# Reordering TensorE's work inside a pipelined local attention: value projection, output product and query turns

## The chip, the core and the metric

The kernel runs on one core of one Trainium2 chip. The metric is the device time of a whole execution in microseconds (us). Inside the core, TensorE (PE, with its weight loads shown apart as PEld), VectorE (DVE), ScalarE (ACT) and GpSimd (POOL) each run their own instruction stream in order and wait for one another only through counting semaphores. SyncE (SP) issues the transfers.

## The reference

An array x of 16 sequences of 256 tokens with 128 channels passes through four residual blocks: a linear attention, a block "ffn", a column attention, and the "ffn" block again with the same weights. Each is applied to a layer norm of x. The changed code is in the "ffn" block, which is two layers deep (so four such layers run, n = 0 to 3):

```
for l in range(DEPTH):                       # DEPTH = 2
    h = shift_token(x)
    q, k, v = split(h @ wqkv)                # 8 heads of 64
    q, k = l2norm(q) * qs, l2norm(k) * ksc
    q, k = rotary_xpos(q, k)
    o = local_attention(q, k, v)             # windows of 64 tokens, each sees itself and the one before
    x = x + o @ wo
    h = layernorm(shift_token(x)) * lg + lb
    a, g = split(h @ w1 + b1)
    x = x + (a * gelu(g)) @ w2 + b2
```

## The kernel before

Each of the four layers first runs its token attention (`attention_programs`) and then its gated part (`gated_programs`). The attention works through 32 tiles. For projection, a tile is 128 tokens with all 8 heads; for attention itself, tile i is a pair of heads (c = i % 4) of a pair of sequences (p = i // 4). Each engine has a hand-written loop over i in which tile i is in one phase and later tiles are in earlier phases (LEAD = 5, LATE = 27). In one pass of TensorE's loop:

- `query_key(i + 5)`: queries and keys of a later tile projected into the two banks `proj`, three products each.
- `scores(i)`: masks, then 32 small products (64 x 64 tiles of the array) into the two banks `sc`.
- `values(i + 3)`: the value projection, three products into the bank `ob`. This bank is also where `attend` writes, so `values(i + 3, i)` first waits on `f_ot` until the attention output of tile i - 2 has been copied out of it.
- `turn_probabilities(i - 1)`: eight transposes of the normalised probabilities, four for each half e of the tile (e is one of the two heads), half 0 into `pt[0]` and half 1 into `pt[1]`.
- `project(i - 2)`: the output product with Wo, into the bank `ss`. It needs the same copied output.
- `turn_tile(.., 1)`: keys transposed into `pt[1]`, once ScalarE has copied half 1 of the probabilities from there (`f_p1`).
- `attend(i - 1)`: 24 products of values by probabilities into `ob`, once both halves have been copied (`f_p0` by VectorE, `f_p1` by ScalarE).
- `turn_tile(.., 0)`: queries transposed into `pt[0]`.

In passes with i % 4 == 0, scores come behind values already. In the passes after LATE there is no later tile to project, scores run one tile ahead, and the first steps of the next part (`gate_centre`, `gate_variance`) are woven in.

ScalarE's pass i up to i = 26 is, in program order: squares of the projection (L506), copy of the values (L516), copy of half 1 of the probabilities of tile i - 1 (L916), the eight exponentials of tile i with their sums (L908), copy of the output of tile i - 1 out of `ob` (L922, `f_ot`), copy of the queries (L526), and two short operations for the inverse norms (L926, L930). At i = 27 the copy of the queries comes ahead of that of the output. From i = 29 on the exponentials of tile i and the copy of the output of tile i - 2 come ahead of the copy of the probabilities of tile i - 1.

VectorE's pass holds rotary products (L452, L462), score maxima (L824), the copy of half 0 of the probabilities (L830), sums of squares (L473, L477), the inverse of the softmax sums (L839) and the copy of the keys (L487). GpSimd's pass holds the normalisation of the probabilities (L993), the scaling of queries and keys (L545) and the rotary sums (L536). ScalarE, VectorE and SyncE programs are not part of the diff; GpSimd's `scale` is.

In the layers n = 0 and n = 2 the loop starts at i = -6 with a ramp of projections and turned tiles; in n = 1 and n = 3 this ramp lies in the gated part of the layer before (`early`).

Of the kernel before, what the change touches and what calls it, by code (L numbers as in the profile page):

```python
# [326 lines left out]
TILES = 4 * PAIRS  # L327
LEAD = 5
FIRST, LAST = -LEAD - 1, TILES + 2
LATE = TILES - LEAD  # L330

tokens = lambda t: slice(t * P, (t + 1) * P)
# [101 lines left out]
        split_product(pe, K, banks[w][:], q, t, w).then_inc(S.f_q, 1)  # L434


def transposes(pe, K, n, j, w, bank):

    S = K.s
    pe.wait_ge(S.f_scl, 2 * TILES * n + 2 * j + (2, 1)[w])  # L440
    for c in range(CHUNKS):
        mm = pe.transpose(bank[:, tokens(c)], K.sm[:, j % 2, w, tokens(c)], K.ident[:])  # L442
    mm.then_inc((S.f_ttq, S.f_ttk)[w], 1)
# [92 lines left out]
        pool.tensor_tensor(K.sm[:, r, w], K.m1[:, r, w], K.m2[:, r, w], ALU.add).then_inc(S.f_sum, 1)  # L536


def scale(pool, K, n, j):

    S, r = K.s, j % 2
    for w in (1, 0):
        pool.wait_ge(S.f_sum, 2 * TILES * n + 2 * j + w + 1)
        pool.wait_ge(S.f_rn, TILES * n + j + 1)
        pool.tensor_tensor(heads(K.sm[:, r, w]), heads(K.sm[:, r, w]),  # L545
                           K.rnt[:, r, w * HEADS:(w + 1) * HEADS].unsqueeze(2).broadcast_to([P, HEADS, DH]),
                           ALU.mult).then_inc(S.f_scl, 1)
# [92 lines left out]
def attention_programs(K, n):  # L640

    S = K.s
    pt = K.pt
# [33 lines left out]
    def tensor(pe):  # L677
# [9 lines left out]
        def values(m, i):  # L687
            if m == 0 and begin < 0:
                pe.wait_ge(S.wa_lo, 3 * (n + 1))
                pe.wait_ge(S.ln_nrm, entry + 6)  # L690
            if i >= 2:
                pe.wait_ge(S.f_ot, TILES * n + i - 1)
            elif m >= 1:
                pe.wait_ge(S.f_ve, TILES * n + m)
            split_product(pe, K, K.ob[:], m // 4, m % 4, 2).then_inc(S.f_v, 1)
# [29 lines left out]
                        if s == 1 and w == 2:  # L725
                            mm.then_inc(S.f_sc, 1)

        def turn_probabilities(i):
            for e in range(2):
                pe.wait_ge(S.f_pn, 2 * TILES * n + 2 * i + e + 1)  # L730
                pe.wait_ge((S.f_tq, S.f_tk)[e], TILES * n + min(i + LEAD, TILES))
                for k in range(4):
                    mm = pe.transpose(pt[e][:, tokens(k)], K.prob[:, i % 2, e, k], K.ident[:])  # L733
                mm.then_inc(S.f_pt, 1)

        def attend(i):
            p, c = divmod(i, 4)
# [18 lines left out]
        def turn_tile(i, j, w):  # L756
            if j == 0:
                pe.wait_ge(S.ln_nrm, entry + 5)
            if i >= 1:
                pe.wait_ge((S.f_p0, S.f_p1)[w], TILES * n + i)  # L760
            elif j >= 1:
                pe.wait_ge((S.f_tq, S.f_tk)[w], TILES * n + j)
            transposes(pe, K, n, j, w, pt[w])

        def project(i):
            p, c = divmod(i, 4)
            pe.wait_ge(S.f_ot, TILES * n + i + 1)
            if i == 0:
                pe.wait_ge(S.wa_wo, 16 * (n + 1))
            if c == 0 and p >= 1:  # L770
                pe.wait_ge(S.f_y, PAIRS * n + p)
            pe.matmul(K.ss[:], K.wo[:, c], K.ot[:, c], start=(c == 0), stop=(c == CHUNKS - 1)).then_inc(S.f_wo, 1)  # L772
# [6 lines left out]
        for i in range(begin, LAST):  # L779
            if (1 if begin < 0 else 0) <= i + LEAD < TILES:  # L780
                query_key(pe, K, n, i + LEAD, K.proj)
            if due(i) is not None:
                if due(i) + 2 < PAIRS:
                    centre(due(i) + 2)
                variance(due(i))
            if 0 <= i <= LATE and i % 4:
                scores(i)
            if LATE < i < TILES - 1:
                scores(i + 1)
            if 0 <= i + 3 < TILES:  # L790
                values(i + 3, i)
            if 0 <= i <= LATE and i % 4 == 0:
                scores(i)
            if 1 <= i <= TILES:
                turn_probabilities(i - 1)
            if 2 <= i:
                project(i - 2)
            if 0 <= i + LEAD - 1 < TILES:
                turn_tile(i, i + LEAD - 1, 1)
            if 1 <= i <= TILES:  # L800
                attend(i - 1)
            if 0 <= i + LEAD - 1 < TILES:
                turn_tile(i, i + LEAD - 1, 0)
            if i == LATE:
                scores(i + 1)
            if i == TILES - 2:
                gate_centre(pe, K, n, 0)
            if i == TILES - 1:
                gate_variance(pe, K, n, 0)
                gate_centre(pe, K, n, 1)  # L810
            if i == TILES:
                gate_variance(pe, K, n, 1)
                gate_centre(pe, K, n, 2)
# [174 lines left out]
    def gpsimd(pool):  # L988
        def normalise(i):
            r = i % 2  # L990
            for e in range(2):
                pool.wait_ge(S.f_rd, TILES * n + i + 1)
                pool.tensor_tensor(K.prob[:, r, e], K.prob[:, r, e], K.rden[:, r, e].unsqueeze(2).broadcast_to([P, 4, P]),  # L993
                                   ALU.mult).then_inc(S.f_pn, 1)

        if begin < 0:
            pool.memset(K.ss16[:], NORM_MIN).then_inc(S.f_floor, 1)
            split_value_weights(pool, K, n)
            low_parts(pool, K, n, 1)
        for i in range(begin, LAST):  # L1000
            j = i + LEAD
            if 1 <= i <= TILES:
                normalise(i - 1)
            if 0 <= j - 1 < TILES:
                scale(pool, K, n, j - 1)
            if i % 4 == 1 and 1 <= i and i // 4 + 2 < PAIRS:
                low_parts(pool, K, n, i // 4 + 2)
            if 0 <= j < TILES:
                sums(pool, K, n, j)
            if i == TILES - LEAD:  # L1010
                split_mlp_weights(pool, K, n)
            if i == TILES - 4:
                pool.wait_ge(S.f_sc, 2 * TILES * n + 2 * (TILES - 4))
                pool.wait_ge(S.f_pn, 2 * TILES * n + 2 * i)
                pool.memset(first_rows[:, 0:PAIRS], 0.0).then_inc(S.g_z, 1)
                pool.wait_ge(S.g_z, 2 * n + 1)
            if i == TILES - 1:
                pool.wait_ge(S.f_sc, 2 * TILES * (n + 1))
                pool.wait_ge(S.f_pn, 2 * TILES * n + 2 * i)
                pool.memset(first_rows[:, PAIRS:2 * PAIRS], 0.0).then_inc(S.g_z, 1)  # L1020
                pool.wait_ge(S.g_z, 2 * n + 2)
# [4 lines left out]
def gated_programs(K, n):  # L1026

    S = K.s
# [25 lines left out]
    def gpsimd(pool):  # L1054
        if last:
            for p in range(PAIRS):
                pool.wait_ge(S.f_y, PAIRS * n + p + 1)
                pool.tensor_tensor(K.X[:, pair(p)], K.X[:, pair(p)], K.Y[:, pair(p)], ALU.add).then_inc(S.f_xy, 1)
        if (n + 1) % DEPTH:
            split_query_key_weights(pool, K, n + 1)  # L1060
            low_parts(pool, K, n + 1, 0)
            scale_tables(pool, K, n + 1)
            split_value_weights(pool, K, n + 1)
            for j in range(LEAD):
                if j == 2:
                    low_parts(pool, K, n + 1, 1)
                sums(pool, K, n + 1, j)
                pool.wait_ge(S.f_cl, TILES * (n + 1) + j + 1)
                pool.tensor_tensor(K.rnt[:, j % 2], K.ssc[:], K.mhalf[:].broadcast_to([P, 2 * HEADS]), ALU.pow).then_inc(S.f_rn, 1)
                if j < LEAD - 1:  # L1070
                    scale(pool, K, n + 1, j)

    def tensor(pe):
        def up(x):
# [31 lines left out]
        def early(x):  # L1106
            s, r = divmod(x - 7, 3)
            if r == 0 and 0 <= s < LEAD:
                if s == 0:
                    pe.wait_ge(S.wa_lo, 3 * (n + 1) + 2)  # L1110
                query_key(pe, K, n + 1, s, K.pt)
            if x in (11, 12, 13):
                if x == 11:
                    pe.wait_ge(S.wa_lo, 3 * (n + 2))
                else:
                    pe.wait_ge(S.f_ve, TILES * (n + 1) + x - 11)
                split_product(pe, K, K.ss[:], 0, x - 11, 2).then_inc(S.f_v, 1)
            if 2 <= s < LEAD + 1 and r == 1:
                if s == 2:
                    pe.wait_ge(S.f_ve, TILES * (n + 1) + 3)  # L1120
                else:
                    pe.wait_ge(S.f_tq, TILES * (n + 1) + s - 2)
                transposes(pe, K, n + 1, s - 2, 1, K.ss)
            if 2 <= s < LEAD + 1 and r == 2:
                pe.wait_ge(S.f_tk, TILES * (n + 1) + s - 1)
                transposes(pe, K, n + 1, s - 2, 0, K.ss)

        def turn_output(p):
            pe.wait_ge(S.ff_y, PAIRS * n + p + 1)
# [1268 lines left out]
```

## Time and profile before

| | |
|---|---|
| median of 3 runs | 1757.11 us (1752.05 to 1757.42) |
| the profiled execution | 1754.2 us, span 1752.4 us, mean granted TensorE clock 0.993 |
| busy, share of the span | PE 96%, PEld 62%, DVE 77%, ACT 75%, POOL 64% |
| core of each token attention | tiles 4 to 24, 147.8 to 147.9 us for 20 passes, in each of the four layers |

The span is the time from the first to the last instruction; some 2 us of the execution's time lie around it. The timeline view lists instructions with their start, their duration, the engine, the line, output<-input, and in brackets how long the engine stood idle before and what released it. PE and PEld are two rows of one engine; matmul ends are modelled, so starts are the safer reading.

### The profile page before, as it was taken

How to read it: one execution, taken by the hardware profiler on the slowest of the kernel's cores; microseconds unless marked ns; L12 is line 12 of the kernel's file. 1: busy time of each engine (PE TensorE's matmuls, PEld its weight loads, DVE VectorE, ACT ScalarE, POOL GpSimd, SP SyncE). 2: the span in 40 equal slices, each digit the busy share in tenths (PEclk: the TensorE clock that was granted, in tenths of full speed). 3: DMA queues.
4: the chain of work that ended last, by engine and by line, in shares of the span. 5: the costliest groups of instructions: out<-in, count | busy, mean ns of one | idle time of the engine just before them, and what ended most of it. 6: DMA issues, size and time to landing. Idle time of an engine off the chain costs nothing. (4 is left out here: it accounts for less than half of the span.)

```text
span 1752.4 us, 43496 instructions
## 1 busy us (share of the span) xinstructions
PE 1676.7 (96%) x15560; PEld 1090.1 (62%) x15560; DVE 1342.6 (77%) x2369; ACT 1305.6 (75%) x4472; POOL 1121.3 (64%) x1012
## 2 busy tenths in 40 slices
PE   8998899999989999999899999899999989999999
PEld 5664677775657777554444444577776557777655
DVE  5556898984778988456789887889885678898654
ACT  5445788887358888745799998788887538888863
POOL 5556999992579999703322221899995378999730
PEclk9999999999999999999899999999999999999999
DMA  3001111103011110201665553111102102110111
GB/s 91 2 2 43 27 31 26 26 20 88 13 37 26 32 26 20 56 15 35 124 102 100 104 94 59 48 26 32 26 20 56 52 12 44 26 32 20 44 31 42
DMA packets 67309, 74.90 MB, mean 43 GB/s; under 512 B 13380, under 2 KB 50968, under 8 KB 65048
## 3 DMA queue, kind: packets, MB, share of 16 engines
q1 hardware_dynamic: 67096, 72.13, 19.3%
q8 instruction: 125, 2.05, 0.5%
q14 instruction: 88, 0.72, 0.1%
HBM read 28.08 MB, written 10.49 MB: 22 GB/s over the span
## 5 line engine op out<-in xcount | busy, mean ns | idle before, releaser
L536 POOL TENSOR_TENSOR rsum<-pa,pb 128x512 f32<-128x512 f32 x256 | 325.6, 1292 | 63.8 <-DVE pa L452 42.3
L908 ACT ACTIVATE ffn_prob<-sc,ffn_nmax 128x128 f32<-128x128 f32 x928 | 326.7, 387 | 4.1 <-DVE ffn_nmax L824 4.1
L993 POOL TENSOR_TENSOR ffn_prob<-ffn_prob,ffn_rden 128x512 f32<-128x512 f32 x256 | 265.2, 1057 | 52.0 <-DVE ffn_rden L839 44.5
L545 POOL TENSOR_TENSOR rsum<-rsum,ffn_rnt 128x512 f32<-128x512 f32 x256 | 261.4, 1042 | 8.0 <-ACT ffn_rnt L930 5.7
L462 DVE TENSOR_TENSOR pb<-proj,tab 128x512 f32<-128x512 f32 x236 | 161.9, 686 | 85.8 <-ACT rn L506 85.4
L908 ACT ACTIVATION_READ_ACCUMULATOR ffn_prob<-sc,ffn_nmax 128x1 f32 x928 | 210.3, 227 | 0.0
L442 PE MATMUL pt<-ident,rsum 128*128 128x128 f32 x960 | 154.2, 284 | 10.4 <-POOL rsum L545 7.7
L442 PEld LDWEIGHTS pt<-ident,rsum 128*128 128x128 f32 x960 | 100.7, 141 | 91.8 <-ACT ffn_ptb L916 70.5
L824 DVE TENSOR_REDUCE ffn_nmax<-sc 128x4 f32<-128x512 f32 x232 | 148.6, 682 | 11.8 <-PE sc L723 8.5
L473 DVE TENSOR_REDUCE ffn_ss<-rn 128x16 f32<-128x1024 f32 x128 | 154.7, 1209 | 0.0
L452 DVE TENSOR_TENSOR pa<-proj,tab 128x512 f32<-128x512 f32 x236 | 150.9, 681 | 0.0
L733 PE MATMUL pt<-ident,ffn_prob 128*128 128x128 f32 x1024 | 143.2, 277 | 6.3 <-POOL ffn_prob L993 5.7
L752 PEld LDWEIGHTS ob<-ffn_ptb,ffn_v 128*64 128x64 f32 x3072 | 126.0, 137 | 33.2 <-issue 20.9
L752 PE MATMUL ob<-ffn_ptb,ffn_v 128*64 128x64 f32 (+1 forms) x3072 | 143.6, 243 | 0.0
L733 PEld LDWEIGHTS pt<-ident,ffn_prob 128*128 128x128 f32 x1024 | 115.7, 140 | 39.7 <-POOL ffn_prob L993 24.7
L2072 ACT ACTIVATE column_E<-proj,column_nm 128x256 f32<-128x256 f32 x256 | 122.3, 500 | 16.9 <-DVE column_nm L1966 16.3
L1168 ACT ACTIVATE ffn_prob<-proj,ffn_colb 128x512 f32<-128x512 f32 (+1 forms) x92 | 62.5, 687 | 96.6 <-PE proj L1093 95.4
L772 PE MATMUL ss<-ffn_ot,ffn_wo 128*128 128x512 f32 x256 | 131.9, 597 | 0.8 <-ACT ffn_ot L922 0.8
L1814 POOL CAST column_kh<-column_ks 128x2048 fp32r<-128x2048 f32 x16 | 30.6, 1910 | 150.9 <-DMA column_ks<-qk_parts 141.2
L506 ACT ACTIVATE rn<-proj 128x512 f32<-128x512 f32 x236 | 125.8, 582 | 0.4
L1205 DVE SCALAR_TENSOR_TENSOR ffn_ptb<-sc,ffn_colb,ffn_prob 128x512 f32<-128x512 f32 (+1 forms) x92 | 68.4, 747 | 73.6 <-ACT ffn_prob L1168 66.9
L2072 ACT ACTIVATE column_E<-sc,column_nm 128x256 f32<-128x256 f32 x256 | 123.2, 511 | 0.0
(322 smaller groups left out, 4348.7 us busy)
## 6 DMA issues: line engine op xcount, KB each, us to landing
ffn_v<-ffn_v SPq DMA_DIRECT2D x128, 128.0 KB, 2.3
column_ks<-qk_parts SPq DMA_DIRECT2D x64, 128.0 KB, 4.0
rn<-Y SPq DMA_DIRECT2D x32, 128.0 KB, 2.3
qk_parts<-column_hi SPq DMA_DIRECT2D x64, 64.0 KB, 1.6
qk_parts<-column_lo SPq DMA_DIRECT2D x64, 64.0 KB, 1.6
column_qs<-qk_parts SPq DMA_DIRECT2D x32, 128.0 KB
column_qs<-qk_parts SPq DMA_DIRECT2D x64, 64.0 KB
rn<-Y SPq DMA_DIRECT2D x32, 127.5 KB, 2.4
```

The costliest lines, as they stand in the source:

```text
L442: mm = pe.transpose(bank[:, tokens(c)], K.sm[:, j % 2, w, tokens(c)], K.ident[:])
L452: return dve.tensor_tensor(heads(K.m1[:, r, w]), heads(banks[w][:]), K.tab[:, t % 2, 2 * w].unsqueeze(1).broadcast_to([P, HEADS, DH]), ALU ...
L462: return dve.tensor_tensor(halves(K.m2[:, r, w]), halves(banks[w][:])[:, :, ::-1], K.tab[:, t % 2, 2 * w + 1].rearrange("p (a d) -> p a d" ...
L473: dve.tensor_reduce(K.ss16[:, :, 0], K.sq.rearrange("p w (h d) -> p (w h) d", d=DH), AX.X, ALU.add).then_inc(S.f_ss, 1)
L536: pool.tensor_tensor(K.sm[:, r, w], K.m1[:, r, w], K.m2[:, r, w], ALU.add).then_inc(S.f_sum, 1)
L545: pool.tensor_tensor(heads(K.sm[:, r, w]), heads(K.sm[:, r, w]), K.rnt[:, r, w * HEADS:(w + 1) * HEADS].unsqueeze(2).broadcast_to([P, HEAD ...
L733: mm = pe.transpose(pt[e][:, tokens(k)], K.prob[:, i % 2, e, k], K.ident[:])
L752: mm = pe.matmul(K.ob[e * DH:(e + 1) * DH, s * SEQ + q0:s * SEQ + q1], K.v[:, b, 3 * s + k, hc], K.ptb[:, r, e, blk, q], start=True, stop= ...
L824: dve.tensor_reduce(K.nmax[:, i % 2, e], blocks(score_banks(i)[e][:]), AX.X, ALU.max, negate=True).then_inc(S.f_mx, 1)
L908: ins = act.activation(K.prob[:, r, e, k], score_banks(i)[e][:, tokens(k)], ACT.Exp, bias=K.nmax[:, r, e, k:k + 1], accum_out=K.den[:, r, ...
L993: pool.tensor_tensor(K.prob[:, r, e], K.prob[:, r, e], K.rden[:, r, e].unsqueeze(2).broadcast_to([P, 4, P]), ALU.mult).then_inc(S.f_pn, 1)
L2072: act.activation(B.E[:, slot, bt], score_banks[c][:, bt * SEQ:(bt + 1) * SEQ], ACT.Exp, bias=B.nm[:, slot, bt:bt + 1], accum_out=B.dn[:, s ...
```

## The change

Four orders change, and no operation is added, removed or resized:

- in TensorE's pass, `values` comes ahead of `scores` in every pass, not only when i % 4 == 0 (also ahead of the scores that run one tile ahead behind LATE)
- `turn_probabilities` is cut in two, with `project` between half 0 and half 1
- the queries are turned ahead of `attend`, and the keys behind it (they were the other way round)
- `scale` on GpSimd scales queries before keys in the attention loop, to match; the tiles prepared in the gated part keep keys first, through the new argument `first`

```diff
-def transposes(pe, K, n, j, w, bank):
+def transposes(pe, K, n, j, w, bank, first):
...
-    pe.wait_ge(S.f_scl, 2 * TILES * n + 2 * j + (2, 1)[w])
+    pe.wait_ge(S.f_scl, 2 * TILES * n + 2 * j + (1 if w == first else 2))
...
-def scale(pool, K, n, j):
+def scale(pool, K, n, j, first):
...
-    for w in (1, 0):
+    for w in (first, 1 - first):
...
-        def turn_probabilities(i):
-            for e in range(2):
-                pe.wait_ge(S.f_pn, 2 * TILES * n + 2 * i + e + 1)
-                pe.wait_ge((S.f_tq, S.f_tk)[e], TILES * n + min(i + LEAD, TILES))
-                for k in range(4):
-                    mm = pe.transpose(pt[e][:, tokens(k)], K.prob[:, i % 2, e, k], K.ident[:])
-                mm.then_inc(S.f_pt, 1)
+        def turn_probabilities(i, e):
+            pe.wait_ge(S.f_pn, 2 * TILES * n + 2 * i + e + 1)
+            pe.wait_ge((S.f_tq, S.f_tk)[e], TILES * n + min(i + LEAD, TILES))
+            for k in range(4):
+                mm = pe.transpose(pt[e][:, tokens(k)], K.prob[:, i % 2, e, k], K.ident[:])
+            mm.then_inc(S.f_pt, 1)
...
-            transposes(pe, K, n, j, w, pt[w])
+            transposes(pe, K, n, j, w, pt[w], 0)
...
-            if 0 <= i <= LATE and i % 4:
+            if 0 <= i + 3 < TILES:
+                values(i + 3, i)
+            if 0 <= i <= LATE:
                 scores(i)
             if LATE < i < TILES - 1:
                 scores(i + 1)
-            if 0 <= i + 3 < TILES:
-                values(i + 3, i)
-            if 0 <= i <= LATE and i % 4 == 0:
-                scores(i)
             if 1 <= i <= TILES:
-                turn_probabilities(i - 1)
+                turn_probabilities(i - 1, 0)
             if 2 <= i:
                 project(i - 2)
+            if 1 <= i <= TILES:
+                turn_probabilities(i - 1, 1)
             if 0 <= i + LEAD - 1 < TILES:
-                turn_tile(i, i + LEAD - 1, 1)
+                turn_tile(i, i + LEAD - 1, 0)
             if 1 <= i <= TILES:
                 attend(i - 1)
             if 0 <= i + LEAD - 1 < TILES:
-                turn_tile(i, i + LEAD - 1, 0)
+                turn_tile(i, i + LEAD - 1, 1)
...
-                scale(pool, K, n, j - 1)
+                scale(pool, K, n, j - 1, 0)
...
-                    scale(pool, K, n + 1, j)
+                    scale(pool, K, n + 1, j, 1)
...
-                transposes(pe, K, n + 1, s - 2, 1, K.ss)
+                transposes(pe, K, n + 1, s - 2, 1, K.ss, 1)
...
-                transposes(pe, K, n + 1, s - 2, 0, K.ss)
+                transposes(pe, K, n + 1, s - 2, 0, K.ss, 1)
```

## Rows read from the trace of the kernel before

**Rows 1.** Windows, passes 4 to 24: length, busy PE PEld DVE ACT POOL, PEclk

```profile
215.22:363.06 147.84, 147.84 (x1741) 110.04 (x1740) 132.50 (x231) 127.83 (x481) 137.89 (x125) 1.00 0.12 27
```

**Rows 2.** Waits in the second layer's attention: who for whom, total, times, longest

```profile
PEld pt L442 <- ACT ffn_ptb L916: 12.2, 19, 0.6
ACT ffn_ptb L916 <- PE pt L733: 9.6, 19, 1.0
ACT ffn_v L516 <- PE ob L422: 8.7, 14, 0.6
```

**Rows 3.** Timeline of pass 13 of the second layer, scores ahead of values

```profile
602.48 0.64 ACT L922 COPY ffn_ot<-ob 128x512 f32<-128x512 f32 x1
...
604.72 0.19 PEld L420 LDWEIGHTS ob<-ffn_wv_hi,ffn_hhi 128*128 128x128 f32 x1 [0.17 <-issue]
...
605.06 0.40 PE L421 MATMUL ob<-ffn_wv_lo,ffn_hhi 128*128 128x512 f32 x1
...
605.54 1.04 PE L733 MATMUL pt<-ident,ffn_prob 128*128 128x128 f32 x8
...
606.41 1.02 PE L772 MATMUL ss<-ffn_ot,ffn_wo 128*128 128x512 f32 x2
...
607.25 0.42 PEld L442 LDWEIGHTS pt<-ident,rsum 128*128 128x128 f32 x4 [0.64 <-ACT ffn_ptb L916]
```

**Rows 4.** Timeline of pass 16 of the second layer, values ahead of scores

```profile
624.20 0.19 PEld L420 LDWEIGHTS proj<-wqk_hi,ffn_hhi 128*128 128x128 f32 x1
...
624.77 0.64 ACT L922 COPY ffn_ot<-ob 128x512 f32<-128x512 f32 x1
...
625.47 0.19 PEld L420 LDWEIGHTS ob<-ffn_wv_hi,ffn_hhi 128*128 128x128 f32 x1
...
625.94 0.40 PE L421 MATMUL ob<-ffn_wv_lo,ffn_hhi 128*128 128x512 f32 x1
...
627.71 0.85 PEld L733 LDWEIGHTS pt<-ident,ffn_prob 128*128 128x128 f32 x8 [0.17 <-POOL ffn_prob L993]
...
628.64 1.02 PE L772 MATMUL ss<-ffn_ot,ffn_wo 128*128 128x512 f32 x2
628.84 0.58 ACT L916 COPY ffn_ptb<-pt 128x512 f32<-128x512 f32 x1 [0.96 <-PE pt L733]
629.05 0.68 DVE L830 COPY ffn_ptb<-pt 128x512 f32<-128x512 f32 x1
...
629.48 0.42 PEld L442 LDWEIGHTS pt<-ident,rsum 128*128 128x128 f32 x4 [0.64 <-ACT ffn_ptb L916]
629.50 0.63 PE L442 MATMUL pt<-ident,rsum 128*128 128x128 f32 x4
...
630.06 0.98 PEld L752 LDWEIGHTS ob<-ffn_ptb,ffn_v 128*64 128x64 f32 x24 [0.17 <-issue]
...
631.50 0.19 PEld L420 LDWEIGHTS proj<-wqk_hi,ffn_hhi 128*128 128x128 f32 x1
...
632.07 0.64 ACT L922 COPY ffn_ot<-ob 128x512 f32<-128x512 f32 x1
```

**Rows 5.** Timeline of ScalarE in pass 1 of the second layer

```profile
520.96 0.63 ACT L922 COPY ffn_ot<-ob 128x512 f32<-128x512 f32 x1
```

**Rows 6.** Timeline of the second layer's last passes, 27 to 32

```profile
713.35 0.11 PEld L713 LDWEIGHTS sc<-mask,identb 64*64 64x64 bf16 x4 [1.22 <-ACT ffn_qT L526]
...
717.53 0.58 ACT L916 COPY ffn_ptb<-pt 128x512 f32<-128x512 f32 x1 [0.29 <-PE pt L733]
...
723.50 0.69 ACT L922 COPY ffn_ot<-ob 128x512 f32<-128x512 f32 x1
...
733.11 0.59 ACT L916 COPY ffn_ptb<-pt 128x512 f32<-128x512 f32 x1 [0.15 <-PE pt L733]
...
738.77 0.98 PEld L752 LDWEIGHTS ob<-ffn_ptb,ffn_v 128*64 128x64 f32 x24 [0.76 <-DVE ffn_ptb L830]
```

**Rows 7.** Windows, a stretch of the column attention, same columns

```profile
800.00:900.00 100.00, 90.46 (x484) 42.21 (x484) 73.75 (x148) 77.70 (x278) 35.05 (x28) 0.90 0.49 90
```

## The prediction

> **What bounds the kernel now.** I read the windows over the steady passes first. Twenty passes take 147.84 us in the first layer (147.84 to 147.89 in the others), 7.39 us each, and TensorE's matmul row is busy all of it at full granted clock, while GpSimd is at 93%, VectorE at 90% and ScalarE at 86% [rows 1]. No engine has a tenth to spare, so the kernel is a ring of engines that hand tiles on, and the question is which ring of waits is the longest.
>
> The waits view comes second. The reader sees that TensorE's weight loads wait most for ScalarE's copy of probability half 1 before the keys are turned, and that ScalarE waits for TensorE in two places, 9.6 us before that copy and 8.7 us before the copy of the values [rows 2]. These look like gaps to close. The timeline tells what they are worth. In pass 13 the eight turns start at 605.54, the output product at 606.41 and the keys' load at 607.25 [rows 3]: 0.87 and then 0.84. Pass 16 shows the product followed by the keys' turn after 0.84 as well, with the same 0.64 of load wait [rows 4]. The product itself has two parts whose row of pass 13 is 1.02 long, so the 0.64 lies beside a running product: the weight loader is idle, the array is not. ScalarE's two gaps are off the ring too. TensorE is bound by its own order, and ScalarE's copy lands just in time.
>
> **The slack between the rings.** `values` may start only when the output of the tile before has left `ob`. In pass 13, where scores come first, the output copy ends at 602.48 + 0.64 = 603.12 and the values start at 604.72: 1.6 us of slack [rows 3]. In pass 16, where values already come first, the copy ends at 625.41 and the values start at 625.47 [rows 4]. That is 0.06 us. So the new order of values and scores uses up all the slack that there is, in every pass, though by itself it costs nothing: pass 16 is of that kind now and is not slower.
>
> **The edits one by one.** (Times relative to the load of the first value product, V.)
>
> *Values ahead of scores.* Work on the array is the same. Pass 16 has V at 625.47, the turns of half 0 at 627.71 and all eight turns done when the output product starts at 628.64, so at V + 3.17 [rows 4]. ScalarE gets its values sooner, but it had been waiting there (8.7 us over 14 waits [rows 2]), and behind it waits again for the probabilities. Gain: none.
>
> *Output product between the halves.* Half 0 is unaffected. Half 1 is finished one output product later. Its length is the step from its start to that of the keys' turn, 629.50 - 628.64 = 0.86 [rows 4]. Nothing on TensorE gets longer, but what waits for half 1 is late by 0.86: ScalarE's copy L916 starts 0.20 after the last turn (628.64 to 628.84) [rows 4], so now at V + 3.17 + 0.86 + 0.20 = V + 4.23. Queued behind that copy on ScalarE are the eight exponentials of the next tile and then the copy of the output out of `ob`, and for that one the next `values` waits. The possible gain, that half 1 no longer waits for GpSimd's second normalisation, is small: that wait is 0.17 in its row of pass 16 [rows 4], and the array was draining anyway.
>
> *Queries before, keys behind `attend`.* The queries' turn has to wait for VectorE's copy of half 0, which in pass 16 starts at 629.05, V + 3.58 [rows 4]. `attend` needs ScalarE's copy, done at V + 4.23 + 0.58 = V + 4.81. Before, the whole output product lay in the time between the last turn and this copy; now only the queries' turn (about 0.4) does, and TensorE stands for some 0.3 us. Keys arrive 1.5 us later at VectorE, whose copy of them stands late in its pass behind other work, so that costs nothing; if that cover were gone it would cost up to that 1.5 only in the pass that begins a new group of four heads. `scale` in the other order costs GpSimd the same work; the first half it gives out is the one now wanted first. No transfer is moved past another: SyncE's stores of values follow the values' copy and come a little sooner.
>
> **The ring that closes.** V, then scores, half 0, product, half 1 up to ScalarE's copy: 4.23. Copy and exponentials until the output copy starts: 632.07 - 628.84 = 3.23; the output copy 0.64; its release to TensorE 0.06 (copy of half 1 ends 629.42, the load that it releases is at 629.48) [rows 4]. Together 8.16. When values wait, the array is empty and no load is hidden under another product, yet the second product follows sooner: V to the second value product is 0.34 in pass 13 and 0.47 in pass 16 [rows 3, 4]. That takes 0.13 off: **8.03 us per pass**, against 7.39 now. Before, the way from V to the end of the turns was 1.69 (604.72 to 606.41 [rows 3]) in place of 4.03, so the same ring was 5.8 and never closed. The other engines have room: their work per pass is 6.9 (GpSimd), 6.6 (VectorE) and 6.4 us (ScalarE) [rows 1].
>
> By how many passes: the output copy of pass 1 starts at 520.96 in the second layer [rows 5] and should not move, since half 1 of the first tile waits for GpSimd there. It releases values of pass 2 at about 521.65. Twenty-five turns of 8.03 later, at 722.4, come the values of pass 27. In that pass scores of the next tile wait for the queries' copy, behind the exponentials: 4.10 + 3.23 + 0.63 + 0.05 = 8.01, so at 730.4. They stand at 713.35 [rows 6]. **Loss up to there 17.1 us per layer.**
>
> *The last passes.* From that point on, ScalarE copied half 1 of tile 27 4.18 later; now it is 0.86 (product) and about 0.2 (two more changes between the full array and its 64 x 64 tiles, at 0.17 of idle loads each [rows 3], partly hidden) later. Then 5.97 to the output copy (717.53 to 723.50) [rows 6]. In the old order half 1 was turned by then. Now the output product waits for the output copy and half 1 for the product: 0.69 + 0.05 + 0.86 + 0.44 (four turns) + 0.20 = 2.24 before the next copy of half 1. Two more passes of 2.24 + 3.23 put the copy of half 1 of tile 30 at 24.4 behind the scores, where it is 19.8 now (733.11) [rows 6]: 4.6 later. The last `attend` (738.77) adds 0.4. **Loss 5.0 per layer**; bounds 1.0 (only the product is felt once) to 7.
>
> Sum: (17.1 + 5.0) x 4 = 88. The profiled execution took 1754.2, its span 1752.4; that makes 1842.6. The median of runs is 2.9 above the profiled one, so 1845.
>
> **A rule weighed.** The turns, the copies and the product use three banks. The Trainium skill, Perfetto Trace Analysis, section Optimizing Tensor Performance (Matmuls), says that independent groups should rotate through banks so that the copying of one overlaps the products of the next. The new order does just that between `pt[0]`, `ss` and `pt[1]`, and by the rule alone the 0.64 of load wait would be the gain. The rows say that the array was covered there.
>
> **Rivals.**
> 1. *The order relieves TensorE* (the other side; the rule above speaks for it). ScalarE would not hold the ring, because something in its 3.87 shrinks. Then every pass is like pass 16, 7.30 between its loads of the query projection (624.20 to 631.50 [rows 4]) against 7.39, and GpSimd's late half 1 no longer counts: 0.09 x 25 x 4 = 9 us less, 1748. It decides if the output copy ends less than 1.27 us into the pass (624.20 to 625.47), as now. Against: the copy of half 1 cannot start before half 1 is turned. Chance 0.05.
> 2. *Only `attend` waits, the `ob` ring does not close.* TensorE's order with the wait for half 1: 4.87 to `attend`, 1.44 for it and the turn behind it (630.06 to 631.50), 1.27 for the query projection [rows 4]: 7.58 per pass. 0.19 x 25 x 4 = 19, with the last passes 39: 1796. It decides if exponentials and copies after half 1 take under 3.3 us instead of 3.87. Chance 0.08.
> 3. *Nothing measurable*: the delays fall into ScalarE's two gaps, 1757. They did amount to 18.3 us in 140 us [rows 2], about 1 us per pass, but they stand before the copy that is late, not behind it. Chance 0.03.
> 4. *TensorE's clock drops* in the new gaps. It is granted in full in the steady windows [rows 1], and was granted at 0.90 over 100 us of the column attention [rows 7]. At 0.90 the array's 7.39 becomes 8.2, 0.2 above the ring: 20 more, 1865; at 1.2 GHz throughout it would be far over. Chance 0.04.
>
> **How the numbers follow.** The forecast has 0.80. A measurement of this kernel can tell about 0.3%, 5 us. The ring's own uncertainty is 0.15 us per pass (15 us in all), the last passes' -4 to +2 per layer (-16 to +8): the forecast's range is 1820 to 1868. For 8 in 10 with the rivals I take 1812 to 1868. Faster 0.05, same 0.03, slower 0.92.
>
> **What the profile would show.** The output copy L922 released straight before the first value product, with "ACT ffn_ot" as the releaser of PE's L420, 0.4 to 0.7 us each pass; `attend` (L752's place) waiting some 0.3 for ScalarE's L916; twenty passes in about 160.6 us; TensorE's load share down from 74% to 68%; the gap of ScalarE before its values' copy gone and the one before its copy of half 1 larger. The forecast is wrong if the passes stay under 7.6 us or if TensorE shows no wait on L922.

## The result: 1845.89 us, 5.25% slower

| | median us | range | runs |
|---|---|---|---|
| before | 1754.58 | 1751.97 to 1757.42 | 4 |
| changed | 1845.89 | 1843.94 to 1851.46 | 4 |

The ratio is 1.0525, 95% interval 1.051 to 1.054. The profiled execution of the changed kernel took 1851.46 us (span 1849.7), 5.6 above the median; the section on the hardware tells where that comes from. The kernel before, measured again beside it, has a median of 1754.58, against 1757.11 when the prediction was made.

Lines of the page of the changed kernel (engine totals, then groups of instructions: busy us, mean ns | idle before). From `turn_probabilities` on (L733 in the kernel before) line numbers are one lower in the changed kernel; in the kernels of the experiments they can differ by one or two more.

```profile
PE 1724.2 (93%) x15560; PEld 1100.1 (59%) x15560; DVE 1358.3 (73%) x2369; ACT 1296.6 (70%) x4472; POOL 1123.0 (61%) x1012
...
L915 ACT COPY ffn_ptb<-pt 128x512 f32<-128x512 f32 x128 | 75.0, 586 | 221.9 <-PE pt L732 221.9
...
L771 PE MATMUL ss<-ffn_ot,ffn_wo 128*128 128x512 f32 x256 | 133.5, 603 | 6.2 <-ACT ffn_ot L921 6.2
```

ScalarE stands idle for 221.9 us before its copies of the probabilities, waiting for TensorE's turns, and TensorE's busy share has gone from 96% to 93%.

The window over passes 4 to 24 of the second layer (length, then busy PE, PEld, DVE, ACT, POOL, and PEclk):

```profile
567.23:727.49 160.26, 155.30 (x1740) 110.12 (x1740) 135.71 (x231) 126.24 (x481) 138.32 (x126) 1.00 0.11 25
```

It is 160.26 us against the 147.84 of [rows 1] (first layer; the second layer's passes have the same length): 8.01 us per pass, with the same count of matmuls and weight loads and the clock granted in full. Nothing was added; every engine became idler.

The waits view of the second layer's attention (600 to 740 us: who for whom, total, times, longest):

```profile
ACT ffn_ptb L915 <- PE pt L732: 30.0, 18, 1.7
...
PEld ob L420 <- ACT ffn_ot L921: 8.9, 17, 0.6
...
PEld pt L442 <- DVE ffn_ptb L829: 6.5, 18, 0.4
```

Beside [rows 2], the wait of the values' load (L420) for ScalarE's output copy (L921) is new, 17 times, and the load of the turn behind the halves now waits for VectorE's copy of half 0. ScalarE's wait for the turns has trebled (9.6 to 30.0). The loads' share of the window of twenty passes is 69% where it was 74%.

One sign that the prediction named is missing: `attend` is not listed as waiting for ScalarE. In the timeline below its load (652.11) starts 0.17 behind the queries' loads and 0.08 behind the end of ScalarE's copy (652.03). The wait stands one step earlier, before the queries' turn, and it is for VectorE.

The timeline of one pass of the changed kernel, against [rows 4]:

```profile
647.35 0.19 PEld L420 LDWEIGHTS ob<-ffn_wv_hi,ffn_hhi 128*128 128x128 f32 x1 [0.41 <-ACT ffn_ot L921]
...
647.69 0.40 PE L421 MATMUL ob<-ffn_wv_lo,ffn_hhi 128*128 128x512 f32 x1
...
649.45 0.42 PEld L732 LDWEIGHTS pt<-ident,ffn_prob 128*128 128x128 f32 x4 [0.17 <-issue]
...
649.95 1.02 PE L771 MATMUL ss<-ffn_ot,ffn_wo 128*128 128x512 f32 x2
...
650.79 0.68 DVE L829 COPY ffn_ptb<-pt 128x512 f32<-128x512 f32 x1
650.81 0.60 PE L732 MATMUL pt<-ident,ffn_prob 128*128 128x128 f32 x4
...
651.44 0.59 ACT L915 COPY ffn_ptb<-pt 128x512 f32<-128x512 f32 x1 [1.67 <-PE pt L732]
651.53 0.42 PEld L442 LDWEIGHTS pt<-ident,rsum 128*128 128x128 f32 x4 [0.36 <-DVE ffn_ptb L829]
...
652.11 1.00 PEld L751 LDWEIGHTS ob<-ffn_ptb,ffn_v 128*64 128x64 f32 x24 [0.17 <-issue]
...
653.57 0.19 PEld L420 LDWEIGHTS proj<-wqk_hi,ffn_hhi 128*128 128x128 f32 x1
...
654.67 0.63 ACT L921 COPY ffn_ot<-ob 128x512 f32<-128x512 f32 x1
...
655.36 0.19 PEld L420 LDWEIGHTS ob<-ffn_wv_hi,ffn_hhi 128*128 128x128 f32 x1 [0.56 <-ACT ffn_ot L921]
```

The reader can walk the ring in it. Values start at 647.35. Half 0 is turned from 649.45, the product runs from 649.95, half 1 comes 0.86 behind it (650.81), and ScalarE gets it at 651.44: 4.09 after the values. 3.23 later, at 654.67, the exponentials are through and the output copy starts; it ends at 655.30 and the next values start at 655.36. 4.09 + 3.23 + 0.63 + 0.06 = 8.01.

The last passes of the same layer on ScalarE, against [rows 6]:

```profile
764.86 0.58 ACT L915 COPY ffn_ptb<-pt 128x512 f32<-128x512 f32 x1 [2.51 <-PE pt L732]
...
770.82 0.69 ACT L921 COPY ffn_ot<-ob 128x512 f32<-128x512 f32 x1
773.16 0.58 ACT L915 COPY ffn_ptb<-pt 128x512 f32<-128x512 f32 x1 [1.65 <-PE pt L732]
...
776.39 0.63 ACT L921 COPY ffn_ot<-ob 128x512 f32<-128x512 f32 x1
778.68 0.59 ACT L915 COPY ffn_ptb<-pt 128x512 f32<-128x512 f32 x1 [1.65 <-PE pt L732]
...
784.20 0.58 ACT L915 COPY ffn_ptb<-pt 128x512 f32<-128x512 f32 x1 [1.65 <-PE pt L732]
```

From the copy of half 1 of tile 27 (764.86) to that of tile 30 (784.20) are 19.3 us; before, 717.53 to 733.11 were 15.6 [rows 6].

### The profile page after: what moved, and what is told of

It reads as the page before. It is cut to its first block and busy times, and to the rows that moved or that the text cites. A ratio compares the mean times of both kernels' runs of the same rounds, so it can differ in the third digit from the quotient of the medians.

```text
span 1849.7 us, 43496 instructions
## 1 busy us (share of the span) xinstructions
PE 1724.2 (93%) x15560; PEld 1100.1 (59%) x15560; DVE 1358.3 (73%) x2369; ACT 1296.6 (70%) x4472; POOL 1123.0 (61%) x1012
## 5 line engine op out<-in xcount | busy, mean ns | idle before, releaser
L915 ACT COPY ffn_ptb<-pt 128x512 f32<-128x512 f32 x128 | 75.0, 586 | 221.9 <-PE pt L732 221.9
L732 PEld LDWEIGHTS pt<-ident,ffn_prob 128*128 128x128 f32 x1024 | 119.4, 142 | 94.2 <-issue 86.5
L732 PE MATMUL pt<-ident,ffn_prob 128*128 128x128 f32 x1024 | 162.5, 282 | 1.6 <-POOL ffn_prob L992 1.2
L723 PE MATMUL sc<-ffn_kT,ffn_qT 64*64 64x128 f32 (+1 forms) x3712 | 123.0, 261 | 0.0
```

## The experiments

The three edits on TensorE make eight combinations. All are in the table; six more kernels, told below it, move something else. "Pass" is the mean of 20 passes of the second layer, read from the starts of ScalarE's probability copies or of the values' loads. Ratios are to the kernel before on the same chip, and each profile is of one execution.

| kernel | pass us | median us | ratio (95%) |
|---|---|---|---|
| before | 7.39 | 1754.6 to 1757.1, by comparison | 1 |
| values first | 7.38 | 1755.28 | 1.0003 (0.9988 to 1.0017) |
| queries first | 7.42 | 1758.36 | 1.0008 (0.9998 to 1.0019) |
| values + queries first | 7.61 | 1775.13 | 1.0113 (1.0093 to 1.0133) |
| product between | 8.20 | 1858.79 | 1.0588 (1.0573 to 1.0603) |
| values first + product between | 8.16 | 1860.76 | 1.0606 (1.0577 to 1.0636) |
| product between + queries first | 7.83 | 1819.67 | 1.0361 (1.0337 to 1.0386) |
| all three (the change) | 8.01 | 1845.89 | 1.0525 (1.051 to 1.054) |

The time grows by a smaller share than the pass, since only some 100 of these passes lie in it and the rest of the kernel did not move.

**Values first.** The order of values and scores of the change, with `turn_probabilities` for both halves together and keys ahead of `attend`. Against the changed kernel:

```diff
-            transposes(pe, K, n, j, w, pt[w], 0)
+            transposes(pe, K, n, j, w, pt[w], 1)
...
             if 1 <= i <= TILES:
                 turn_probabilities(i - 1, 0)
+                turn_probabilities(i - 1, 1)
             if 2 <= i:
                 project(i - 2)
-            if 1 <= i <= TILES:
-                turn_probabilities(i - 1, 1)
...
-                turn_tile(i, i + LEAD - 1, 0)
+                turn_tile(i, i + LEAD - 1, 1)
...
-                turn_tile(i, i + LEAD - 1, 1)
+                turn_tile(i, i + LEAD - 1, 0)
...
-                scale(pool, K, n, j - 1, 0)
+                scale(pool, K, n, j - 1, 1)
```

> Only the values go ahead of the scores; both halves are turned together, keys ahead of attend. Theory of the ring (values wait for the output copy, which waits for the exponentials and for half 1): without the product in front of half 1 the ring is 3.17 + 0.20 + 3.23 + 0.64 + 0.06 = 7.30 us per pass, just what TensorE needs in pass 16, so no loss: 1745 to 1757 us. Rival, that this edit alone brings the waits for the bank: values wait 0.4 us or more in each pass, 1795 us or more.

1755.28 us, no difference. The passes are 7.30, 7.30, 7.62 and 7.30. The ring of 7.30 just fits; the 7.62 stands where GpSimd also splits an input (L554) and the turn of half 1 waits 0.36 for GpSimd's normalisation.

**Product between.** Of the change only the product between the halves stays. Scores come ahead of values as before (i % 4 != 0), and keys ahead of `attend`. Against the changed kernel:

```diff
-            transposes(pe, K, n, j, w, pt[w], 0)
+            transposes(pe, K, n, j, w, pt[w], 1)
...
-            if 0 <= i + 3 < TILES:
-                values(i + 3, i)
-            if 0 <= i <= LATE:
+            if 0 <= i <= LATE and i % 4:
                 scores(i)
             if LATE < i < TILES - 1:
                 scores(i + 1)
+            if 0 <= i + 3 < TILES:
+                values(i + 3, i)
+            if 0 <= i <= LATE and i % 4 == 0:
+                scores(i)
...
-                turn_tile(i, i + LEAD - 1, 0)
+                turn_tile(i, i + LEAD - 1, 1)
...
-                turn_tile(i, i + LEAD - 1, 1)
+                turn_tile(i, i + LEAD - 1, 0)
...
-                scale(pool, K, n, j - 1, 0)
+                scale(pool, K, n, j - 1, 1)
```

> Only the output product goes between the halves; scores ahead of values and keys ahead of attend, as before. Theory of the ring: the ring from values to values is 2.55 + 0.20 + 3.23 + 0.64 + 0.06 = 6.7 us and stays open, so values wait for nothing. But the keys wait for the copy of half 1, and the product no longer lies in that time: half 1 is turned 5.33 us into the pass, copied at 6.17, then keys 0.44 + 0.13, attend 1.05, queries 0.41: 8.2 us per pass, 0.8 x 25 x 4 = 81 and 20 for the last passes, about 1855 us. Rival, that this edit costs only through the ring: 7.39 us per pass, 1757 to 1777 us.

1858.79 us, 8.20 per pass: this edit alone is dearer than all three. The weight loads of this kernel:

```profile
646.63 0.42 PEld L442 LDWEIGHTS pt<-ident,rsum 128*128 128x128 f32 x4 [0.91 <-ACT ffn_ptb L917]
...
648.65 0.19 PEld L420 LDWEIGHTS proj<-wqk_hi,ffn_hhi 128*128 128x128 f32 x1
...
654.85 0.42 PEld L442 LDWEIGHTS pt<-ident,rsum 128*128 128x128 f32 x4 [0.91 <-ACT ffn_ptb L917]
```

The keys' loads wait 0.91 for ScalarE's copy, 17 times, 0.7 of it with the array idle too, and no value load waits for the output copy. 8.22 separate the two loads of the keys.

**Queries first.** Scores ahead of values, both halves together, and the exchange of queries and keys with the order of scaling (the change's own lines for `turn_tile` and `scale`).

> Only the queries go ahead of attend and the keys behind it (with the order of scaling). Theory: the product still covers the copy of half 1, and the queries need VectorE's copy of half 0, which was there in time: no wait, 7.39 us per pass or a little less, 1745 to 1757 us. Rival, that keys are late for VectorE or for the scores of the next group of heads: up to 1 us in each fourth pass, 7 x 4 of them, 1765 to 1785 us.

1758.36 us, no difference. Every fourth step is 7.66: in the pass where values come first as well, the queries' load waits 0.95 for VectorE's copy of half 0. The other three are 7.32, 7.42 and 7.26.

**Output copied midway.** The changed kernel with ScalarE's output copy between the exponentials of half 0 and half 1:

```diff
                 ins.then_inc(S.f_ex, 1)
+                if e == 0 and 1 <= i < LATE:
+                    keep_output(i - 1)
...
-            if 1 <= i < LATE:
-                keep_output(i - 1)
```

> The changed kernel, with one line of ScalarE moved: the output copy stands between the exponentials of half 0 and of half 1 (passes 1 to 26), so it is 1.4 us earlier; nothing on TensorE moves. Theory of the ring: the ring falls to 6.7 us and opens, values wait for nothing, what stays is attend's wait for half 1: 7.58 us per pass, and 20 us of the last passes: about 1796 us. Rival, that the loss lies in TensorE's order (attend, changes of tile size) and the wait of values is only where it shows: 1840 to 1850 us as in the changed kernel.

1837.93 us (ratio 1.0453, 1.0431 to 1.0475). Neither number: 7.92 per pass in the mean, in steps of 7.90, 8.23, 7.62 and 7.93. The timeline of this kernel:

```profile
644.99 0.42 PEld L442 LDWEIGHTS pt<-ident,rsum 128*128 128x128 f32 x4 [0.66 <-DVE ffn_ptb L829]
...
645.58 0.98 PEld L751 LDWEIGHTS ob<-ffn_ptb,ffn_v 128*64 128x64 f32 x24 [0.17 <-issue]
...
646.75 0.59 ACT L923 COPY ffn_ot<-ob 128x512 f32<-128x512 f32 x1
...
648.29 0.19 PEld L420 LDWEIGHTS ob<-ffn_wv_hi,ffn_hhi 128*128 128x128 f32 x1
...
652.89 0.42 PEld L442 LDWEIGHTS pt<-ident,rsum 128*128 128x128 f32 x4 [0.66 <-DVE ffn_ptb L829]
```

The values' load at 648.29 has no wait on ScalarE any more, so the ring did open. But the queries' load now waits 0.66 for VectorE (L829), and the output copy starts only when `attend` has ended. I had built another ring: output copy, exponentials of half 1, queries' copy, inverse norms, squares, VectorE's maxima and its copy of half 0, queries' turn, `attend`, output copy: 646.75 to 654.65 in the trace, 7.90 us. What makes the neighbouring steps longer and shorter was not followed. The run shows that the wait of values goes, but not what the pass would be with nothing in its place.

**Product between and queries first.** The changed kernel with the old condition for scores and values.

> The changed kernel with values behind scores again, as before the change; product between the halves and queries ahead of attend stay. Theory of two waits: without values ahead of scores the ring through the bank is 6.7 us and open; attend still waits for the copy of half 1 at 6.17, so 6.17 + 1.05 + 0.41 = 7.63 us per pass: 1757 + 0.24 x 25 x 4 + 20 = about 1801 us. Rival: values ahead cost nothing, as they cost nothing alone, so 1840 to 1850 us.

1819.67 us. It is some 26 us faster than the full change, so values first, which alone costs nothing, costs 26 us here. It is 18 us above my sum because the steps are 7.68, 8.01, 7.69 and 7.91 in place of 7.63. Every fourth pass has values ahead of scores already, and there the ring closes at its 8.01 (values wait 0.32 for the output copy), which I had not counted. The 7.91 has no such wait. In it, as in every second pass, the queries' loads wait 0.62 for VectorE's copy of half 0, 0.4 of it with the array idle; that was not counted either.

**Values and queries first.** The changed kernel with `turn_probabilities` for both halves together ahead of `project`.

> The changed kernel with the output product behind both halves again; values ahead of scores and queries ahead of attend stay. Theory: half 1 is turned at V + 3.17, the ring is 7.30 us and TensorE needs 7.30 to 7.39: 1745 to 1757 us, no measurable difference from the kernel before or a shade faster. Rival, that the loss needs only values first and the late keys: above 1775 us.

1775.13 us: neither theory, but clear of the kernel before. The loads of this kernel:

```profile
648.04 0.19 PEld L420 LDWEIGHTS ob<-ffn_wv_hi,ffn_hhi 128*128 128x128 f32 x1
...
651.09 0.30 PEld L771 LDWEIGHTS ss<-ffn_ot,ffn_wo 128*128 128x128 f32 x2
652.34 0.42 PEld L442 LDWEIGHTS pt<-ident,rsum 128*128 128x128 f32 x4 [0.95 <-DVE ffn_ptb L828]
...
655.64 0.19 PEld L420 LDWEIGHTS ob<-ffn_wv_hi,ffn_hhi 128*128 128x128 f32 x1
```

The queries' load waits 0.95, against 0.64 that the product covers, and the pass is 7.60 (648.04 to 655.64). VectorE can take the maxima only when the scores are there, 0.7 us later than where scores come first, and copies half 0 behind them; in this kernel its maxima (L822) wait for the scores 16 times in 140 us, 7.9 us in all. In the prediction I had seen that this copy starts at V + 3.58, and priced it at nothing, because the copy of half 1 was later still.

**Old turns at the end.** The changed kernel, but from pass 28 on both halves are turned ahead of the product:

```diff
-            if 2 <= i:
+            if 2 <= i <= LATE:
                 project(i - 2)
             if 1 <= i <= TILES:
                 turn_probabilities(i - 1, 1)
+            if LATE < i:
+                project(i - 2)
```

> The changed kernel, but from pass 28 on the output product stands behind both halves. Theory: the 5 us per layer of the last passes go, 25 passes of 8.0 us stay: 20 us less than the changed kernel, 1826 us. Rival: the last passes are bound by something else (exponentials, gate), 1840 to 1846 us.

1825.32 us (ratio 1.0397, 1.0368 to 1.0427), some 21 below the changed kernel. The time from the probability copy of tile 26 to that of tile 31 falls from 34.06 to 28.85 us; before it was 28.58.

**Queries copied first, on the changed kernel and on the kernel before.** The work stays, and only the order of two ScalarE copies is swapped:

```diff
-            if 1 <= i < LATE:
-                keep_output(i - 1)
             if 0 <= j - 1 < TILES:
                 keep_queries(act, K, n, j - 1, pt[0])
+            if 1 <= i < LATE:
+                keep_output(i - 1)
```

> The changed kernel with two copies of ScalarE swapped in each pass: the queries' copy (0.46 us from start to start) ahead of the output copy. No engine gets more work. Theory: the output copy stands on the ring, so every pass is 0.46 longer, 8.48 us: 46 us more than the changed kernel, about 1892 us. Rival, that TensorE's own order sets the pass and the wait of values is a by-product: within 5 us of the changed kernel.

On the changed kernel 1895.14 us (ratio 1.0792, 1.0759 to 1.0825), 8.50 per pass. Its timeline:

```profile
641.03 0.63 ACT L526 COPY ffn_qT<-pt 128x512 f32<-128x512 f32 x1
...
641.50 0.65 ACT L921 COPY ffn_ot<-ob 128x512 f32<-128x512 f32 x1
...
642.20 0.19 PEld L420 LDWEIGHTS ob<-ffn_wv_hi,ffn_hhi 128*128 128x128 f32 x1 [1.05 <-ACT ffn_ot L921]
...
646.30 0.59 ACT L915 COPY ffn_ptb<-pt 128x512 f32<-128x512 f32 x1 [2.15 <-PE pt L732]
...
650.70 0.19 PEld L420 LDWEIGHTS ob<-ffn_wv_hi,ffn_hhi 128*128 128x128 f32 x1 [1.05 <-ACT ffn_ot L921]
```

The output copy starts 0.47 behind the queries' copy, the values' load waits 1.05 for it, and from values to values it is 642.20 to 650.70 = 8.50, so 0.49 longer than in the changed kernel.

> The kernel before with the same swap of two ScalarE copies as in the run on the changed kernel. Theory of slack: where scores come ahead of values the output copy has 1.6 us to spare, so 0.46 later costs nothing; only in each fourth pass, where values come first, it costs 0.4: 0.4 x 7 x 4 = 11, about 1768 us. Rival, that a later output copy costs 0.46 in every pass whatever the order (ScalarE's order is bound): 1803 us.

On the kernel before 1765.02 us (ratio 1.0058, 1.0045 to 1.0071). Its loads of values:

```profile
626.58 0.19 PEld L420 LDWEIGHTS ob<-ffn_wv_hi,ffn_hhi 128*128 128x128 f32 x1 [0.17 <-issue]
632.88 0.19 PEld L420 LDWEIGHTS ob<-ffn_wv_hi,ffn_hhi 128*128 128x128 f32 x1 [0.52 <-ACT ffn_ot L922]
641.59 0.19 PEld L420 LDWEIGHTS ob<-ffn_wv_hi,ffn_hhi 128*128 128x128 f32 x1 [0.17 <-issue]
```

Only the values of each fourth pass wait for the output copy. The step to them grows from 5.82 to 6.30, and the next one gives 0.13 back. So the same half microsecond costs 47 to 49 us (by ratios, by medians) on one kernel and 10 on the other.

**Values first and product between.** The changed kernel with keys ahead of `attend` and queries behind it.

> The changed kernel with keys ahead of attend and queries behind it again: values first and product between the halves only. Theory: half 1 is turned 1.27 + 4.03 = 5.30 us into the pass, copied at 6.14; only then keys 0.58, attend 1.05, queries 0.38: 8.15 us per pass, above the ring's 8.01, with the last passes about 1855 us. Rival, that the ring through the bank sets the pass whatever is behind the halves: 8.01 us, 1843 to 1847 us.

1860.76 us, 8.16 per pass, equal in every pass. By these sums, of two waits the longer decides: 8.15 for keys and `attend` in a row behind half 1, against the ring's 8.01. So the exchange of queries and keys, alone worth nothing, gives 15 us back in the change.

**Halves swapped.** The changed kernel with TensorE untouched; ScalarE and VectorE exchange the halves that they copy:

```diff
-            dve.wait_ge(S.f_pt, 2 * TILES * n + 2 * i + 1)
+            dve.wait_ge(S.f_pt, 2 * TILES * n + 2 * i + 2)
...
-            dve.tensor_copy(K.ptb[:, i % 2, 0], blocks(pt[0][:])).then_inc(S.f_p0, 1)
+            dve.tensor_copy(K.ptb[:, i % 2, 1], blocks(pt[1][:])).then_inc(S.f_p1, 1)
...
-            act.wait_ge(S.f_pt, 2 * TILES * n + 2 * i + 2)
+            act.wait_ge(S.f_pt, 2 * TILES * n + 2 * i + 1)
...
-            act.copy(K.ptb[:, i % 2, 1], blocks(pt[1][:])).then_inc(S.f_p1, 1)
+            act.copy(K.ptb[:, i % 2, 0], blocks(pt[0][:])).then_inc(S.f_p0, 1)
```

> The changed kernel, TensorE untouched, but ScalarE copies half 0 and VectorE half 1. Work is the same on each engine. Theory of the ring: ScalarE's copy, exponentials and output copy now hang on half 0, turned 1.3 us before half 1, so the ring falls to 6.7 us and opens; attend waits for VectorE's copy of half 1 at V + 4.75: 4.75 + 1.44 + 1.27 = 7.46 us per pass, and most of the last passes' loss goes too: 1765 to 1775 us. Rival, that the product between the halves costs by itself, whoever copies: 1840 us or more.

1814.98 us (ratio 1.0347, 1.0331 to 1.0363), 31 faster than the change and 40 above the upper end of what I expected. Its timeline:

```profile
644.49 0.19 PEld L420 LDWEIGHTS ob<-ffn_wv_hi,ffn_hhi 128*128 128x128 f32 x1
...
647.50 0.59 ACT L915 COPY ffn_ptb<-pt 128x512 f32<-128x512 f32 x1 [0.54 <-PE pt L732]
...
648.16 0.60 PE L732 MATMUL pt<-ident,ffn_prob 128*128 128x128 f32 x4
...
648.79 0.69 DVE L829 COPY ffn_ptb<-pt 128x512 f32<-128x512 f32 x1 [0.57 <-PE pt L732]
...
649.55 1.01 PEld L751 LDWEIGHTS ob<-ffn_ptb,ffn_v 128*64 128x64 f32 x24 [0.60 <-issue]
...
650.74 0.62 ACT L921 COPY ffn_ot<-ob 128x512 f32<-128x512 f32 x1
...
652.29 0.19 PEld L420 LDWEIGHTS ob<-ffn_wv_hi,ffn_hhi 128*128 128x128 f32 x1
```

The ring is open: the output copy ends at 650.74 + 0.62 = 651.36, 0.9 us before the values' load. This pass is 7.80 (644.49 to 652.29), the mean of twenty 7.78, and the rows give my error. Half 1 is turned by V + 4.10, VectorE starts 0.20 later and takes 0.69, so `attend` begins at V + 5.06; I had left out the 0.20 and taken ScalarE's shorter copy. With 1.47 to the next query projection and 1.27 to the values the sum is 7.80. The other part of the miss is the last passes. I had expected most of their loss to go, and none of it did: from the probability copy of tile 26 to that of tile 31 are 33.99 us, against 34.06 in the changed kernel.

**Values and queries first, halves swapped.** The kernel of "values and queries first" with the swap just shown.

> Values first and queries ahead of attend, both halves turned together, and ScalarE copies half 0, VectorE half 1. Theory: the queries' wait for VectorE's copy (7.61 us per pass in the run with both edits) goes, since ScalarE has copied half 0 by V + 3.5; VectorE's copy of half 1 ends at V + 4.25, behind the queries' turn: 7.30 to 7.39 us per pass, 1745 to 1757 us. Rival, that the wait moves on to attend: above 1765 us.

1752.31 us (ratio 0.9984, 0.9975 to 0.9993): passes of 7.27, 7.27, 7.27 and 7.66, mean 7.37. It is the fastest of all and its interval lies just below 1, a gain smaller than the 0.3% that the prediction took as what can be told. The wait for VectorE's copy of half 0 (0.22 us in each pass, 20 us in all) is gone.

## Why the prediction was right

**The ring.** Forecast 8.03 us per pass, measured 8.01. Its terms: 4.10 to ScalarE's copy (4.09), 3.23 (3.23), 0.64 (0.63), 0.06 (0.06). That it is this ring, and not only a wait that shows, rests on the swap of the two copies: 0.47 more on one link made every pass 0.49 longer, at the same work. On the kernel before, whose ring was priced at 5.8 with slack everywhere but in each fourth pass, the same swap costs only there.

The 0.86 for the product, by which half 1 is late, was read from a step whose end was also a wait for ScalarE's copy [rows 4]. That was not safe, but it held: in the changed kernel, where the next turn waits for no other engine, the step is 0.86 as well (649.95 to 650.81).

**Where it starts and ends.** Delay in front of the last passes 17.1 forecast; the probability copy of tile 26 of the second layer moves from 709.43 to 755.63, 46.20, of which 29.25 were there when the layer's values began (507.77 to 537.02): 16.95. The last passes cost 5.2 in the run that undoes them (34.06 against 28.85), forecast 5.0. The whole second layer lost 22.3 (its last `attend` moved 51.57, less 29.25), forecast 22.1. The sum of 1845 stands beside 1845.89, and that it is this near is in part luck. The forecast loss was 88, the measured one 91.3, and the prediction started from a median of 1757.11 where the one measured beside the change is 1754.58.

**The edits one by one.** Values first: nothing gained and nothing lost alone, as said. Product between: the culprit, as said, through half 1 being late by one product. But the prediction tells only one of the two costs of this edit. Without the other edits the ring stays open and the edit costs more (8.20), because the keys and `attend` both stand behind the late copy. The queries' turn, which the prediction priced as leaving TensorE a stall of 0.3, is what shortens this second path to less than the ring.

**What was mis-sized.** VectorE's copy of half 0 was put at nothing. In the change that holds for the time: the queries' turn does wait for it (0.36 of load wait), but ScalarE's copy, on which the ring hangs, does not. The stall of 0.3 that the prediction put before `attend` is not there in the rows. Without the product between it is 0.22 us in each pass (7.61 against 7.39), 20 us: the change would have been slower even without its dear edit. And the price of 7.58 for a pass with the ring opened (second rival) was never met: the two kernels that opened it came to 7.92 and 7.78, each held by a path that the opening itself made or lengthened. What a pass would be with values in a bank of their own no run shows; the banks `proj` (two), `sc` (two), `pt` (two), `ob` and `ss` all have their work.

**The rivals.** Relief of TensorE: ruled out as to the whole change; the 0.64 of load wait before the keys was covered by the product, and where the product was moved away it became 0.91, 0.7 of it with the array idle (product between). The bank-rotation rule of the Trainium skill (Perfetto Trace Analysis, Optimizing Tensor Performance) is what the product between the halves does, and the runs decide against its use here (1858.79 us for this edit alone): it overlaps a copy with a product, but the other half's copy, for which the ring and the keys wait, comes later by that product. Only `attend` waits: that is the neighbour of the change (7.68 in the passes of "product between and queries first" that have scores first). Delays that vanish in ScalarE's gaps: the gaps before the copy grew from 9.6 to 30.0 us instead. The clock: it fell briefly, see below.

## What to carry over

When engines are all nearly full, follow one item around the loop and add durations and hand-overs between two uses of the same buffer; the loop with the largest sum sets the pass, whatever the busy shares are. An instruction moved ahead of another at no cost in work is free only up to the slack of every loop through what it delays, and two edits that are each free can use up the same slack together. Before trusting a fix that opens one loop, price the next one: in these kernels three of them, of 8.15, 8.01 and 7.90 us, lie within 0.3 us of each other.

## What the runs showed of the hardware

In the profiled execution of the changed kernel TensorE's clock was not granted in full in three stretches of these layers (windows: length, busy PE, PEld, DVE, ACT, POOL, then PEclk):

```profile
160.00:200.00 40.00, 34.47 (x195) 22.20 (x193) 32.94 (x54) 27.52 (x68) 31.29 (x28) 0.91 0.22 53
420.00:430.00 10.00, 7.23 (x70) 4.78 (x70) 2.89 (x6) 6.98 (x38) 4.07 (x4) 0.64 0.23 55
1380.00:1410.00 30.00, 24.59 (x313) 17.77 (x312) 13.63 (x24) 19.11 (x82) 16.53 (x17) 0.89 0.23 54
```

The profiled execution of the kernel before had 1.00 over 160 to 200, and over 390 to 420 and 1320 to 1350, its own last passes of the first and third layer.

The first stretch is not the change's doing. It lies in the ramp, ahead of the first probability copy at 199.96 us, and it is there as well in the kernel before with the queries copied first, whose ramp is the old one: 0.84 over 160 to 170 and 0.85 over 180 to 190, first copy at 199.75.

The second lies in the first layer's last passes. At 424.57 the two parts of an output product took 2.08 us together, against 1.02 elsewhere, so the engine ran at 1.2 in place of 2.4 GHz. Over 410 to 420, ahead of the fall, it was 75% busy at a clock of 1.00, with waits of 0.2 to 1.5 us between groups. Seven of the kernels have the product between the halves in their last passes, and the profiles of four show such a fall at the end of the first layer (over the worst ten microseconds 0.64, 0.67, 0.64 and 0.83); of the seven with the old last passes none does. With one profile of each that speaks for the new gaps as its cause but does not show it.

The third stretch lies at the end of the third layer's attention, where one pass took 9.64 us in place of 8.02. The first layer lost 25.6 us from its first to its last probability copy and the third 24.1, where the second lost 22.4 and the fourth 22.5. The other three executions, at a mean clock of 0.991 to 0.992 against 0.987, were 5 to 8 us shorter. So the clock took some 5 us of the profiled execution in the attention layers and a few more in the ramp, and less in the others.
